# Which wait rides on the instruction: TensorE, GpSimd and SyncE in a graph attention kernel

## The reference

```python
q_i = Q[edge_type, dst]
k_j = K[edge_type, src]
v_j = V[edge_type, src]
score = jnp.sum(q_i * k_j, axis=-1) * scale
seg = dst * R + edge_type
m = jax.ops.segment_max(score, seg, num_segments=N * R)
e = jnp.exp(score - m[seg])
s = jax.ops.segment_sum(e, seg, num_segments=N * R)
alpha = e / s[seg]
out = jax.ops.segment_sum(v_j * alpha[..., None], dst, num_segments=N)
return out.reshape(N, HD) + bias
...
x = _layernorm(x + _L0_gnn_ref(x, edge_index, edge_type_5, ...), axis=-1)
```

## Time and profile before

| | us |
|---|---|
| three runs, median | 2276.77 |
| three runs, lowest and highest | 2274.12, 2283.94 |
| the profiled execution | 2263.78 |
| its span, first to last instruction | 2262.0 |

### The profile page before, as it was taken

How to read it: one execution, slowest core, us unless ns; L and a number is a source line. 1 busy time by engine, 2 the same in 40 slices (tenths; PEclk the granted TensorE clock), 3 DMA queues, 4 the chain that set the end, 5 groups by cost and what they waited for, 6 DMA issues and landing times.

```text
span 2262.0 us, 33259 instructions
## 1 busy us (share of the span) xinstructions
PE 1719.4 (76%) x7549; PEld 1186.0 (52%) x7549; DVE 1569.7 (69%) x3858; ACT 1074.7 (48%) x4050; POOL 1176.7 (52%) x1254
## 2 busy tenths in 40 slices
PE   8999995227999995477777777777777777677788
PEld 4555542002444442356666566665666666566667
DVE  8888983002434442587788888887888888888877
ACT  3333320001000000066777777777777777777775
POOL 3111117773666304556666666666666666666504
PEclk9999997657999997699899999999999999999998
DMA  8998737775999747888888889888888998888733
GB/s 225 275 246 226 217 119 231 229 222 185 313 338 329 260 159 234 265 275 265 268 279 282 281 283 283 279 288 281 277 281 286 279 285 284 276 272 278 235 99 114
DMA packets 344898, 571.56 MB, mean 253 GB/s; under 512 B 44993, under 2 KB 238433, under 8 KB 344702
## 3 DMA queue, kind: packets, MB, share of 16 engines
q0 software_dynamic: 87360, 274.23, 40.8%
q1 hardware_dynamic: 224330, 234.48, 31.7%
q10 hardware_dynamic: 33012, 60.73, 7.5%
HBM read 408.84 MB, written 140.96 MB: 243 GB/s over the span
## 4 chain that ended last, share of the span: by engine, by line
PE 53%; DVE 18%; issue 16%; another core or an unknown queue 8%; ACT 3%; POOL 1%; DVEq 1%; DMA 1%; SPq 0%; ACTq 0%; POOLq 0%
PE sums L727 20%; PE sums L796 15%; PE pairs L807 12%; DVE region L1122 3%; DVE region L1323 3%; DVE region L1380 2%; PE bank L762 2%; PE bank L755 1%; DVE region L1332 1%; PE sums L854 1%; POOL region L555 1%; PE sums L865 1%; DVE region L1333 1%; DVE region L1389 1%
## 5 line engine op out<-in xcount | busy, mean ns | idle before, releaser
L555 POOL DMA_INDIRECT region<-kv_tab,kvidx x824 | 806.0, 978 | 566.5 <-issue 198.2
L727 PE MATMUL sums<-region,acc 128*128 128x512 f32 (+2 forms) x1568 | 677.8, 584 | 6.5 <-ACT acc L879 4.1
L994 ACT ACTIVATE region<-region 128x64 f32<-128x64 f32 x2368 | 655.5, 346 | 0.9
L796 PE MATMUL sums<-region 128*128 128x150 f32 x3296 | 500.4, 306 | 129.9 <-issue 125.1
L807 PE MATMUL pairs<-region 128*128 128x256 f32 x1648 | 426.1, 403 | 186.1 <-DVE region L1323 103.4
L796 PEld LDWEIGHTS sums<-region 128*128 128x128 f32 x3296 | 461.4, 199 | 188.6 <-issue 175.6
L727 PEld LDWEIGHTS sums<-region,acc 128*128 128x128 f32 (+1 forms) x1568 | 297.6, 195 | 306.7 <-issue 286.7
L807 PEld LDWEIGHTS pairs<-region 128*128 128x128 f32 x1648 | 312.5, 199 | 249.6 <-issue 210.1
L1291 DVE TENSOR_TENSOR region<-sums,region 128x512 f32<-128x512 f32 (+1 forms) x215 | 147.4, 691 | 368.2 <-PE sums L727 146.2
L1012 ACT COPY acc<-sums 128x294 f32 x824 | 327.2, 397 | 73.5 <-PE sums L796 47.4
L537 POOL DMA_INDIRECT region<-q_tab,region x288 | 274.8, 954 | 147.7 <-issue 81.0
(11 more groups left out here) (244 smaller groups left out, 967.6 us busy)
## 6 DMA issues: line engine op xcount, KB each, us to landing
region<-q_seg SPq DMA_DIRECT2D x824, 128.0 KB
kv_tab<-region ACTq DMA_DIRECT2D x42, 1280.0 KB
q_seg<-region SPq DMA_DIRECT2D x288, 128.0 KB
q_tab<-region SPq DMA_DIRECT2D x48, 640.0 KB, 4.3
region<-rel_tab SPq DMA_DIRECT2D x206, 128.0 KB
region<-region POOLq DMA_DIRECT2D x47, 384.0 KB, 5.5
region<-kv_tab,kvidx POOLq DMA_INDIRECT x824
region<-in_x SPq DMA_DIRECT2D x96, 128.0 KB, 2.8
```

The costliest lines, as they stand in the source:

```text
L555: pool.indirect_dma_start(ring_row[:, a:a + 2 * C], None, kv_tab, bass.IndirectOffsetOnAxis(ap=kvidx[:, t:t + 1], axis=0)).then_inc(s_got[ ...
L727: done = nc.tensor.matmul(bank[o % 4][0:n, 0:w], acc[:, k, t * P:t * P + n], w_sb[:, k, :, :].rearrange("p u c -> p (u c)")[:, c0:c0 + w], ...
L796: done = nc.tensor.matmul(bank[i][:, h * W:(h + 1) * W], ring_v[:, i, spot(q), h * P:(h + 1) * P], oneh[:, q % 2, i, :], start=True, stop= ...
L994: done = nc.scalar.activation(ring_v[:, i, spot(q), h * D:(h + 1) * D], ring_v[:, i, spot(q), h * D:(h + 1) * D], ACT.Copy, scale=alT[:, h ...
```

## The change

Waits that stood as `wait_ge` ahead of an instruction are attached to that instruction with `wait_op`: on TensorE those for an evicted bank (L727), for taken columns (L796) and for the product (L807); on GpSimd those for stored rows (L537) and for the product (L555); on SyncE three of its own. The text of VectorE and ScalarE is the same. `evicted(o)` gives the semaphore and value that `wait_evicted` waited for.

```diff
         def wait_evicted(eng, o):
-            if o < OA:
-                eng.wait_ge(s_evA, o + 1)
-            else:
-                eng.wait_ge(s_evD, o - OA + 1)
+            eng.wait_ge(*evicted(o))
...
-                if j >= PQ:
-                    pool.wait_ge(s_pqout[j % PQ], 16 * (j // PQ))
-                pool.indirect_dma_start(pq[:, j % PQ, :], None, q_tab,
-                                        bass.IndirectOffsetOnAxis(ap=seg_list[:, j:j + 1], axis=0)
-                                        ).then_inc(s_pq[j % PQ], 16)
+                rows_in = pool.indirect_dma_start(pq[:, j % PQ, :], None, q_tab,
+                                                  bass.IndirectOffsetOnAxis(ap=seg_list[:, j:j + 1], axis=0)
+                                                  ).then_inc(s_pq[j % PQ], 16)
+                if j >= PQ:
+                    rows_in.wait_op(s_pqout[j % PQ], 16 * (j // PQ), "sem-ge")
...
-                if s >= KL:
-
-                    pool.wait_ge(s_mul, s - KL + 1)
...
+                    if i == 0 and s >= KL:
+
+                        rows_in.wait_op(s_mul, s - KL + 1, "sem-ge")
...
-                sp.wait_ge(s_pq[j % PQ], 16 * (j // PQ + 1))
-                sp.dma_start(q_seg_rows[j // RB, j % RB], pq[:, j % PQ, :]).then_inc(s_pqout[j % PQ], 16)
+                sp.dma_start(q_seg_rows[j // RB, j % RB], pq[:, j % PQ, :]
+                             ).then_inc(s_pqout[j % PQ], 16).wait_op(s_pq[j % PQ], 16 * (j // PQ + 1), "sem-ge")
...
+                    ranks_in.wait_op(s_lift, s - QS + 1, "sem-ge")
...
-                if o >= 4:
-                    wait_evicted(pe, o - 4)
                 for k in range(KC):
...
+                    if k == 0 and o >= 4:
+                        done.wait_op(*evicted(o - 4), "sem-ge")
...
-                    if q > 0:
-
-                        pe.wait_ge(s_cols, columns_taken(q - 1, i))
...
+                        if h == 0 and q > 0:
+
+                            done.wait_op(s_cols, columns_taken(q - 1, i), "sem-ge")
...
-                if s > 0:
-                    pe.wait_ge(s_mul, s)
                 for i in range(SB):
                     done = nc.tensor.matmul(qk[:, i, :], oht[:, s % 2, i * P:(i + 1) * P], qring[:, s % QS, i, :],
                                             start=True, stop=True)
+                    if i == 0 and s > 0:
+                        done.wait_op(s_mul, s, "sem-ge")
```

More of the change, by code:

```diff
@@ L369, in chunk, with evicted @@
             return (o - NOQ) // R, (o - NOQ) % R * CH, CH
+        def evicted(o):
+            return (s_evA, o + 1) if o < OA else (s_evD, o - OA + 1)
         def wait_evicted(eng, o):
-            if o < OA:
-                eng.wait_ge(s_evA, o + 1)
-            else:
-                eng.wait_ge(s_evD, o - OA + 1)
+            eng.wait_ge(*evicted(o))
         def gathered(s):
@@ L554, in _ @@
                     a = (i * KS + spot(s)) * C
-                    pool.indirect_dma_start(ring_row[:, a:a + 2 * C], None, kv_tab,
-                                            bass.IndirectOffsetOnAxis(ap=kvidx[:, t:t + 1], axis=0)
-                                            ).then_inc(s_got[s % KL], 16)
+                    rows_in = pool.indirect_dma_start(ring_row[:, a:a + 2 * C], None, kv_tab,
+                                                      bass.IndirectOffsetOnAxis(ap=kvidx[:, t:t + 1], axis=0)
+                                                      ).then_inc(s_got[s % KL], 16)
+                    if i == 0 and s >= KL:
+                        rows_in.wait_op(s_mul, s - KL + 1, "sem-ge")
             pool.wait_ge(s_lift, NSB)
@@ L623, in _ @@
             for s in range(NSB):
+                ranks_in = sp.dma_start(
+                    bcr[:, s % QS, :],
+                    rel_rows[s * SB * P:(s + 1) * SB * P].rearrange("(o w) -> o w", o=1).broadcast_to([P, SB * P])
+                ).then_inc(s_rel[s % QS], 16)
                 if s >= QS:
[L626 to L629, removed]
+                    ranks_in.wait_op(s_lift, s - QS + 1, "sem-ge")
                 _, at = nc.values_load_multi_w_load_instructions(
```

## The result

The changed kernel takes 2383.68 us (median of four runs, 2374.62 to 2387.22), the kernel before 2277.84 us in the same comparison (2274.12 to 2283.94). The ratio is 1.0454, with a 95% interval of 1.0433 to 1.0474: 105.8 us slower. The profiled execution of the change took 2374.62 us, its span is 2372.8 us.

A forecast was written before the change was run, and what follows sets the result against it. A ring of hand-overs with single waits, no engine full, was taken to bound the edge stage. TensorE's lifts (3.0 us) and aggregations (2.5) gave about -5: 2258.8 us from the profiled run, 2272 from the median; range 2257 to 2286.

The forecast's parts named there:

- SyncE's part: Edited SyncE transfers: each has its wait on itself in both programs, so 0 us.
- the query gathers: GpSimd's 179 query gathers: starts later by 3.1 us at most, beside the projection, so cost 0.
- the projection: TensorE's projection (L727): bound 2.4 us either way, taken as 0 because TensorE's queue of matmuls hides it.
- TensorE's latencies: TensorE's weight loads: 0.05 us behind a late product instead of 0.11, and 0.05 instead of 0.07 behind L1020.
- the -5 us of the sum: TensorE's gain on the path: 3.0 us from lifts and 2.5 from first aggregations, -5.5 us, taken as -5.
- net 6.3 us lost on GpSimd. That is hidden: GpSimd's edge gathers: 8.6 us lost, 2.3 won, at TensorE's 0.06 us each; hidden by GpSimd's idle time and lead.
- 143 that lose and 39 that win: Edge-gather starts on GpSimd: 143 ended by the aggregation or something unnamed lose, 39 ended by the product win.
- about 30 us: Edge gathers on GpSimd: said to run five steps ahead of VectorE's product, a lead of about 30 us.
- GpSimd becomes late: Rival, first gather of each step: 143 x 0.18 = 26 us, less 7 for the products, +19; time 2291; chance 0.12.
- point of decision: Lateness on GpSimd decides once gathers no longer land before the product; the product's unnamed waits, 30.0 us, would grow.
- the late completions go: Rival, ScalarE's waits before L971 and L985: TensorE's completions 0.3 to 1 us earlier, 14 to 46 us faster; chance 0.11.
- The clock: Rival, edge-stage rounds: TensorE's lower granted clock can move the time by 5 us at most, 0.2 us x 25 rounds.

The follow-up runs named there:

- lift_only: Kernel before with only the lift's swap (L807), s_mul riding; 2278.99 us, ratio 0.9995.
- lift_agg: Kernel before with the swaps at the lifts (L807) and the first aggregation (L796); 2277.44 us, ratio 0.9995.
- ready_rides_again: Kernel before with s_agg ahead on its own instruction, fulfilled s_ready riding on the first edge gather, s_mul not waited for from step 18; 2374.80 us, ratio 1.0423.
- iota run: Kernel before plus an unused 128x128 iota on GpSimd, carrying s_agg, before the first edge gather of 188 steps; 2343.23 us, ratio 1.0344.
- pool_only: Kernel before with only both GpSimd swaps (L537, L555), TensorE as before; 2380.79 us, ratio 1.0444.

## Why the prediction was wrong

*What held.* The change swaps which wait rides; SyncE's part, the query gathers and the projection came to nothing that can be measured. TensorE's latencies were as forecast. After:

```profile
1500.28 1.18 DVE L1325 TENSOR_TENSOR region<-region,pairs 128x1024 f32<-128x1024 f32 x1
...
1501.52 1.60 PEld L807 LDWEIGHTS pairs<-region 128*128 128x128 f32 x8 [0.42 <-DVE region L1325]
```

From the product's end at 1501.46 to the lift is 0.06 us, against 0.11. By the nanosecond it is 0.052 to 0.054 us in 117 of 118 lifts ahead of which the weight loads had been idle for over 0.1 us, against 0.115 or 0.116 in all 118 before. That the end gains from it was wrong or too small to see (lift_only 0.9995, lift_agg 0.9995); the -5 us of the sum are nowhere.

*The step that failed: "net 6.3 us lost on GpSimd. That is hidden".* Both halves were wrong. The price was taken from TensorE, 0.06 us, with 0.18 as the far end in the rival. GpSimd's own is 0.48 us, eight times as much, and I had no row for it. The number of starts was also wrong: I counted 143 that lose and 39 that win, because the profile named the product at 39 starts. The runs show no such gain: with the product's wait gone altogether (ready_rides_again) the loss is the same. 188 x 0.48 = 90.2 us of the 105.8 need no such gain.

The second half took GpSimd's 258.12 busy us of 400 for spare time. The iota run showed that it is none: 0.49 us of lateness a step made the end 0.42 us a step later. The trace of before has a sign of it. The busy and idle times of any engine add up to the period, so the sum says nothing; what speaks is how even the idle time is. These are the first gathers of four steps:

```profile
1501.23 0.95 POOL L555 DMA_INDIRECT region<-kv_tab,kvidx  x1 [1.24 <-PE sums L796]
...
1507.29 0.94 POOL L555 DMA_INDIRECT region<-kv_tab,kvidx  x1 [1.36 <-PE sums L796]
...
1513.38 0.95 POOL L555 DMA_INDIRECT region<-kv_tab,kvidx  x1 [0.95 <-remote]
...
1519.54 0.95 POOL L555 DMA_INDIRECT region<-kv_tab,kvidx  x1 [1.21 <-PE sums L796]
```

A reserve would vary from step to step and touch zero. Here 184 of 188 steps have one pause over 0.7 us, eight in ten of these first pauses are 1.06 to 1.38 us long, and three steps have none.

The "about 30 us" of lead was wrong as well. From a step's first gather to its product it is 16.2 us in the median of before (least 13.0), because the wait for the aggregation holds the gathers back. It was enough for the product even so.

*The rival "GpSimd becomes late" had the place and the sign, but its point of decision was wrong.* I wrote that it decides when gathers no longer land before the product. The product did not wait for them, and the loss came. Priced with 0.48 us for 143 starts, less the 7 us, the rival's own formula gives 62 us; for all 188, and without the 7, it is 90 of the 105.8 us.

*A sign that misled.* I had said that I would be wrong if ScalarE's waits before L971 and L985 shrank by more than 10 us. Those before L971 did, from 71.0 + 2.0 us to the 43.2 of L973 after it (30.5 and 12.4 below, and 0.3), while others grew, the unnamed ones before L947 (after: L949) from 12.2 to 74.1 us. The waits changed place and the time went up, so a shrinking wait alone was no sign of the rival "the late completions go".

```profile
ACT region L949 <- remote: 74.1, 14, 5.8
...
ACT region L973 <- remote: 30.5, 11, 6.4
...
ACT region L973 <- PE bank L777: 12.4, 8, 1.6
```

*The clock.* I gave it 5 us at most. These are stretches of eight steps, product to product: before, then pool_only four times (length, busy us of TensorE, weight loads, VectorE, ScalarE, GpSimd, granted clock, DMA share, GB/s).

```profile
1317.10:1365.36 48.26, 36.16 (x208) 30.67 (x206) 40.80 (x118) 36.21 (x145) 31.42 (x32) 0.96 0.90 282
```

```profile
1461.80:1513.78 51.98, 36.27 (x207) 30.73 (x206) 40.82 (x117) 36.33 (x145) 32.24 (x33) 0.97 0.83 264
1621.03:1675.74 54.71, 39.67 (x208) 34.88 (x206) 40.92 (x118) 36.86 (x145) 31.91 (x33) 0.88 0.80 251
1855.95:1905.71 49.76, 38.96 (x198) 33.50 (x198) 40.76 (x117) 36.04 (x145) 29.53 (x30) 0.86 0.83 259
1905.71:1961.23 55.52, 37.44 (x217) 31.44 (x215) 40.82 (x117) 36.74 (x147) 34.58 (x35) 0.97 0.82 261
```

At a like clock the round is 51.98 in place of 48.26 us, 3.7 us longer, and 8 x 0.48 = 3.8. The second of pool_only has the same work at a granted clock of 0.88 (more of it at 1.2 in place of 2.4 GHz) and is another 2.7 us longer. The last two go the other way, 49.76 us at 0.86 and 55.52 at 0.97; they hold unequal work (198 and 217 matmuls). Over all 158 stretches of eight steps from the 33rd step on, pool_only's length and clock do go together: the correlation is -0.51, and a line through them falls by 1.8 us for each 0.1 of clock. In lift_only, which takes as long as the kernel before, it is -0.21 and 0.2 us. The trace of before has one round that is slow at a low clock too, which the earlier trace rows had not shown:

```profile
1084.91:1137.11 52.20, 39.71 (x206) 34.81 (x206) 40.75 (x116) 35.70 (x142) 31.71 (x32) 0.87 0.84 256
```

So in the changed kernel long rounds and low clocks come together. Whether the clock made them longer, or fell because TensorE idled longer in them, no run separates. The 15.6 us that are left of 105.8 - 90.2 may be the clock's, which is argued and not shown, and so is the split itself.

*What stays open.* The runs show that the end follows GpSimd's lateness nearly one for one (0.42 of 0.49 us), that gathers are in time for the product, and that GpSimd's pause before each step's first gather doesn't depend on which completion it asks for. They don't show what makes the pause, nor by which path a later gather moves the end when no product waits for it. One lead: the other engines also hear from TensorE late, and in the same pauses. After:

```profile
1500.98 0.20 PE L764 MATMUL bank<-ident,region 1*128 1x1 f32 x1
...
1501.42 0.95 POOL L553 DMA_INDIRECT region<-kv_tab,kvidx  x1 [0.30 <-issue]
...
1503.46 0.16 ACT L953 COPY region<-bank 128x2 f32<-128x2 f32 x1 [1.71 <-remote]
...
1504.13 1.14 POOL L553 DMA_INDIRECT region<-kv_tab,kvidx  x1 [1.77 <-remote]
```

L764 ends at 1501.18, GpSimd's last gather of the step at 1502.37, and only at 1503.46 does ScalarE, idle for 1.71 us, start its copy. If completions are held while gathers are issued, a burst that starts 0.48 us later moves every engine by that, whatever the product's lead. A run with fills put between the gathers (spell_in_burst) was meant to test this and fell on a chip without pauses, so the mechanism is a theory. Why chips differ by 16%, and why the pauses show only where the kernel is slower, was not found either.

## What to carry to other kernels

Which of several waits rides on an instruction was worth nothing where they were all fulfilled when the engine came to them, and 0.48 us a step on GpSimd's indirect gathers where it idled for the one put ahead. There, let the wait that comes last ride. Before you call an engine hidden because it is 65% busy, look at its idle times: if one comes back in nearly every step at nearly one length, suspect that the engine is part of the cycle, and test it by adding a piece of work there. A price read on one engine is no bound for another.

## What the hardware showed that I had not expected

- From a completion to the first gather: 0.272 us if the wait rides, 0.752 us if it stands on a semaphore instruction ahead. For an iota on GpSimd with the wait riding it was 0.07 us, for TensorE's weight loads 0.05 and 0.11 us. The Trainium skill (Perfetto Trace Analysis, "Per-instruction lifecycle") has the sequencer decode and push an instruction before its wait begins in the wait queue. The traces agree as far as they go: the wait ahead costs 0.48 us more, and the 0.30 us between two gathers hid three fills, so GpSimd is free in them. That they are work of the issue, and that such work comes after the completion where the wait stands ahead, is a reading that no run measured apart.
- The same program took 2264 to 2279 us on some chips and 1919 us on others. On the latter VectorE is busy 98% of the steady stage, GpSimd issues gathers without a pause, the granted clock is 1.00, DMA moves 328 in place of 282 GB/s, and the change, of which the edge gathers' part was tried there, costs nothing. What lost 4% on one chip lost nothing on the next.
- Three fills of 128x1 between two gathers cost 0.02 us.
